# Two engine orders rewritten: gathers behind the products at a unit's begin, and the last tile's down product by halves

## The chip, the cores and the metric

The kernel runs on one core of one Trainium2 chip. The metric is the device time of one execution in microseconds; before the change it is 761.45, the median of three runs (758.97 to 761.66). The engines are TensorE (PE, whose weight loads are shown as PEld), VectorE (DVE), ScalarE (ACT), GpSimd (POOL) and SyncE (SP, which here only issues transfers).

## What is computed

The input X has 4 sequences of 2048 rows and 256 channels. Cut to what matters:

```python
xp = (X @ Wp + bp).reshape(B, T, 4, D)
f = (pos @ Wf + bf).reshape(T, 3, D)            # filters, from sines and cosines of the position
y = xp[:, :, 0]
for i in range(3):
    y = causal_fft_convolution(y, f[:, i]) * xp[:, :, i + 1]
x = layernorm(X + y)
h = silu(x @ wg.T) * (x @ wu.T)                 # weights are int32, scaled by 1/127
out = layernorm(x + h @ wd.T)
```

## The kernel before, in words

Time is cut into 16 blocks of 128 rows. **Projection**: 128 products (`project`, L398), 64 for each half of the output columns; DVE takes each out of PSUM (`collect`, L793 to L811), ScalarE and POOL split the inputs into a high and a low part. The gates of the three stages go to HBM and come back as tiles (`load_gate`).

**Convolution**: 12 units u (3 stages of 4 groups of 64 channels), each a loop over 16 blocks k (L549 for PE, L734 for ACT, L968 for DVE, L1062 for POOL). A convolution is a Toeplitz product within a block (`toeplitz`, L432 to L434, 8 groups q per unit, each in two halves of 12 small products), done one unit ahead, and a part from all earlier blocks: `state` (L411, three fp16 matmuls, accumulating over the blocks), `multiply` on DVE (L832, state times the filter's coefficients, into `prod`), and `readout` on PE (L452, four fp32 passes). `gather` on DVE (L857) adds two readouts to `y` and frees their PSUM bank; a unit has 8 gathers, numbered 0 to 7, and the last (of one block only) is number 7. `readout` of an odd block waits for the gather that frees its bank (`z_done`). `apply` on POOL (L1033) multiplies `y` by the gate, 9 times a unit. ScalarE makes the scaled copies of the next unit (`high`, L628 and L630), takes out Toeplitz results (`evacuate`, L636) and sums squares (`square`, L643) for the scale of a later unit; DVE makes the low fp16 half (`low`, L866) and, at block 3, the scale itself (`factors`, L815 to L824). PE's Toeplitz group q of the next unit waits for `low` of q and, at every even q, for the filter tile that SP loads (`load_filter`, L264, 1 MB, three slots).

The order of the work is written out by hand for each engine, and every engine runs its list in order. What each list has at a unit's begin: on PE at block 0 the last half Toeplitz group, state 0, readout 15 of the unit before; at block 1 state 1, a half group and the norm; at block 2 a half group, state 2, readout 1. On DVE gather 6 of the unit before comes at block 1 and gather 7 at block 3, both behind the multiply (L974 and L975), except in the last unit and behind it, where they come first in blocks 0 and 1. POOL's `apply` of the unit before follows the same places, and its first one of the new unit stands at block 4. SP's list per unit, for j = 0 to 3: a filter load that waits for a Toeplitz group, then the gate load of the next unit, which waits for squares at blocks 10 and 14 of this unit and 2 and 6 of the next (units 8 on: for `apply`, `gated`). In the unit before the last SP also loads the weights of the feed-forward part and the rows for the first addition.

At the end of the projection DVE's list is: collect 125, multiply 2 of unit 0, collect 126, collect 127; the first `low` of unit 1 follows as the first thing of the unit loop. Projections cycle through PSUM banks 2 to 5, of which readouts use 4 and 5.

**Feed-forward**: 16 tiles of 512 rows (128 rows of each of 4 sequences), 6 hidden blocks m each: gate and up product (L472), `silu` on ACT, `product` on DVE (L905), `high_h` on ACT, `low_h` on POOL (L1052), then the down product. For the last tile `down_last` (L499) loops over m outside and the four sequences b inside; its two halves (b 0 and 1, b 2 and 3) are in two banks and signal `d_done` as block 5 of each is through. Behind it DVE has, for each half, `sum2_half` (L910), `bn_stats` and `bn_aggr`; POOL's `root` (L1040) adds epsilon, negates the mean, takes the power -0.5 and multiplies; three rows are then normalised on ACT (L674), the last on DVE (L1020), and two transfers store the halves.

Of the kernel before, what the change touches and what calls it, by code (L numbers as in the profile page):

```python
# [11 lines left out]
ALU = mybir.AluOpType  # L12
# [3 lines left out]
NB, T, D = 4, 2048, 256  # L16
NS = 3
NA = T // P
# [4 lines left out]
NU = NS * NG  # L23
# [4 lines left out]
NPAIR = NA // 2  # L28
# [8 lines left out]
HM = HID // P  # L37
NTOK = NB * P
NSEG = 8
EPS = 1e-5  # L40
# [5 lines left out]
def program(nc, XT, X, WP, BP, WF, BFC, BFR, POSR, CM, CB, EF, EI, ONES, IDENT, WGT, WUT, WDT, OUT):  # L46
# [3 lines left out]
    with ExitStack() as ctx:  # L50
# [3 lines left out]
        def sem(name):  # L54
            return ctx.enter_context(nc.semaphore(name))
# [17 lines left out]
        mv = sb("mv", [P, 2, NB, 2])  # L73
# [116 lines left out]
        root_ready = sem("root_ready")  # L190
        rstd = sem("rstd")
        const_ready = sem("const_ready")
        x1n_ready = sem("x1n_ready")
        tr_done = sem("tr_done")
        xh_ready = sem("xh_ready")
# [57 lines left out]
        with nc.Block() as block:  # L253
# [134 lines left out]
            def _(pe):  # L388
# [54 lines left out]
                def readout(u, a):  # L443
                    n = u * NE + a - 1
                    m = u * NPAIR + (a - 1) // 2
                    e0 = NA - 1 - a if turned(u // NG) else a
                    half = (a - 1) % 2
                    if half == 0 and m >= 2:
                        pe.wait_ge(z_done, m - 1)
                    pe.wait_ge(mult_done, n + 1)  # L450
                    for h in range(2):
                        mm = pe.matmul(b_out[m % 2][:, half * W:(half + 1) * W], ei[:, h, e0 * P:(e0 + 1) * P],  # L452
                                       prod[:, n % 3, h, :], start=(h == 0), stop=(h == 1))
                    mm.then_inc(r_done, 1)
# [43 lines left out]

                def down_last(k):  # L499
                    pe.wait_ge(zz_ready, k * 2 + 1)  # L500
                    for m in range(HM):
                        pe.wait_ge(hh_ready, k * HM + m + 1)
                        if m < HM - 1:
                            pe.wait_ge(hl_ready, k * HM + m + 1)
                        else:
                            pe.wait_ge(hl_last, 1)
                        for b in range(NB):
                            for h in (hh, hl):
                                mm = pe.matmul(b_d[b // 2][:, (b % 2) * D:(b % 2 + 1) * D],  # L509
                                               h[:, k % 2, m, b * P:(b + 1) * P], wd[:, m, :],  # L510
                                               start=(m == 0 and h is hh and b % 2 == 0),
                                               stop=(m == HM - 1 and h is hl), skip_group_check=True)
                            if m == HM - 1 and b % 2:
                                mm.then_inc(d_done, 1)
# [272 lines left out]
            def _(dve):  # L787
# [166 lines left out]
                for n in range(NT):  # L954
                    collect(NT + n)
                    if n == 6:
                        factors(0)
                    if n == 9:
                        factors(1)
                    if n % 6 == 4 and 1 <= n // 6 <= NQ:  # L960
                        low(0, n // 6 - 1)
                    if n == 56:
                        dve.wait_ge(wfx_ready, 4 * NS)
                    if n in (57, 59, 61):
                        multiply(0, (n - 57) // 2)
                dve.wait_ge(x_lo, 2 * NT)
                dve.wait_ge(wfx_ready, 4 * NS)
                for u in range(NU + 1):  # L968
                    for k in range(NA):
                        if u >= NU - 1 and k <= 1:  # L970
                            gather(u - 1, NPAIR - 2 + k)
                        if k >= 5 and k % 2 and u < NU:
                            gather(u, (k - 5) // 2)
                        if k % 2 == 0 and u + 1 < NU:  # L974
                            low(u + 1, k // 2)  # L975
                        if u < NU and k < NE and (u or k >= 3):
                            multiply(u, k)
                        if k in (1, 3) and 1 <= u < NU - 1:
                            gather(u - 1, NPAIR - 2 + k // 2)
                        if k == 3 and u + 2 < NU:  # L980
                            factors(u + 2)
                        if u == NU - 1:
# [24 lines left out]
                for h in range(2):  # L1007
# [7 lines left out]
                    for b in (2 * h, 2 * h + 1):  # L1015
                        last = nc.vector.bn_aggr(mv[:, 0, b, :], bst[:, 0, b, :])
                    last.then_inc(mean_ready, 1)
                dve.wait_ge(rstd, 2 * NA + 1)
                dve.wait_ge(out_done[1], (NA // 2 - 1) * 16)
                nc.vector.tensor_scalar(oo[:, 1, NB - 1, :], zl[:, NB - 1, :], rs[:, 0, NB - 1:NB], nb[:, 0, NB - 1:NB],  # L1020
                                        ALU.mult, ALU.add).then_inc(oo_last, 1)

            @block.gpsimd
            def _(pool):
# [36 lines left out]
                                            ALU.subtract).then_inc(x_lo, 1)  # L1061
                for u in range(NU + 1):  # L1062
                    for k in range(NA):
                        if u >= NU - 1 and k <= 1:
                            apply(u - 1, NPAIR - 1 + k)
                        if k in (1, 3) and 1 <= u < NU - 1:
                            apply(u - 1, NPAIR - 1 + k // 2)
                        if k == (4 if u < NU - 1 else 2) and u < NU:
                            apply(u, 0)
                        if k >= 5 and k % 2 and u < NU:  # L1070
                            apply(u, (k - 3) // 2)
# [24 lines left out]
                        low_h(k, 5)  # L1096
                pool.wait_ge(oo_ready, (NA - 2) * NB + 1)
                root(1, count2(NA - 1))
                root(0, 2 * NA, slice(0, 2))
                root(0, 2 * NA + 1, slice(2, 4))  # L1100


def tables():
# [60 lines left out]
```

## Time and profile before

| | |
|---|---|
| median of three runs | 761.45 us |
| profiled execution | 759.56 us |
| its span, first to last instruction | 757.8 us |
| mean granted clock of PE | 0.994 of full |
| projection, units, feed-forward in the span | 0 to 200, 200 to 500, 500 to 758 |

How to read it: times in rows are microseconds from the span's start. A row of a timeline has start, duration, engine, line, operation, output and inputs with their sizes, a count, and in brackets the idle time before it with what ended it. PE rows show matmuls whose ends are modelled: their starts are good, their durations overlap. A clock of 1.00 is the upper of PE's two levels (2.4 GHz), 0.50 the lower (1.2 GHz).

### The profile page before, as it was taken

The numbers are of one execution on the slowest core, as the hardware profiler recorded it, in microseconds if no ns is written. First come the engines' busy times: TensorE is split into PE (matmuls) and PEld (weight loads), VectorE is DVE, ScalarE is ACT, GpSimd is POOL, SyncE is SP. The second block draws the span as 40 slices with busy tenths as digits, with TensorE's granted clock in tenths as the row PEclk, the third lists the DMA queues.
The fourth block names the chain that finished last, engine by engine and source line by source line (L and its number), as shares of the span: only waits on it lengthen the run. The fifth ranks groups of instructions, "written<-read, shape, count | busy, mean of one in ns | idle before, by whom it ended". The sixth has DMA issues, their size and how long they took to land.

```text
span 757.8 us, 16074 instructions
## 1 busy us (share of the span) xinstructions
PE 732.5 (97%) x5936; PEld 547.3 (72%) x5936; DVE 552.1 (73%) x1083; ACT 488.0 (64%) x962; POOL 421.3 (56%) x483
## 2 busy tenths in 40 slices
PE   6999999999999999999999999799999999999995
PEld 5878878888788888888888888555665556655663
DVE  4898778777788888888888888766656566565644
ACT  3445554444378888788877665456677776777753
POOL 3445554445244443444444434798788878888653
PEclk9999999999999999999999999999999999999998
DMA  8659668999899998999899996622435435442322
GB/s 301 214 177 337 241 216 283 317 319 309 278 277 263 256 267 245 260 258 262 250 247 270 304 264 212 225 57 57 108 88 123 101 89 108 95 128 57 64 55 78
DMA packets 193676, 152.69 MB, mean 202 GB/s; under 512 B 35776, under 2 KB 177216, under 8 KB 193344
## 3 DMA queue, kind: packets, MB, share of 16 engines
q1 hardware_dynamic: 191744, 146.36, 66.6%
q10 hardware_dynamic: 1856, 5.31, 2.1%
q8 instruction: 48, 0.79, 0.4%
q14 instruction: 28, 0.23, 0.1%
HBM read 109.45 MB, written 34.34 MB: 190 GB/s over the span
## 4 chain that ended last, share of the span: by engine, by line
PE 88%; DVE 4%; DMA 3%; ACT 2%; issue 2%; POOL 1%; SPq 0%; POOLq 0%; DVEq 0%; ACTq 0%
PE bank L398 22%; PE bank L472 21%; PE bank L452 19%; PE bank L493 10%; PE bank L411 7%; PE bank L432 3%; PE bank L433 3%; PE bank L434 3%; DMA toep<-filter_rows 1%; DMA wi<-in_WDT 1%; DVE y L857 1%; PE bank L509 1%; DVE wfx L844 1%; DVE prod L832 1%; DMA xt<-in_XT 1%
## 5 line engine op out<-in xcount | busy, mean ns | idle before, releaser
L1033 POOL TENSOR_TENSOR y<-y,gate 128x512 f32<-128x512 f32 (+1 forms) x108 | 124.4, 1157 | 170.2 <-DVE y L857 157.6
L398 PE MATMUL bank<-wps,xs 128*128 128x512 f32 x768 | 183.5, 398 | 7.8 <-DVE wps L790 6.6
L452 PE MATMUL bank<-prod,ei 128*128 128x256 f32 x720 | 188.0, 384 | 1.5 <-DVE y L857 1.5
L398 PEld LDWEIGHTS bank<-wps,xs 128*128 128x128 f32 x768 | 144.7, 190 | 39.4 <-POOL xs L1060 7.3
L832 DVE TENSOR_TENSOR prod<-bank,wfx 128x512 f32<-128x512 f32 x180 | 124.2, 690 | 43.7 <-PE bank L411 43.7
L1060 POOL TENSOR_TENSOR xs<-xt,xs 128x256 fp32r<-128x256 f32 x128 | 93.5, 742 | 101.2 <-ACT xs L607 101.2
L472 PE MATMUL bank<-xh,wq 128*128 128x512 f16 x384 | 145.7, 379 | 0.3 <-DVE hf L905 0.2
L472 PE MATMUL bank<-xl,wq 128*128 128x512 f16 x384 | 145.8, 380 | 0.0
L1052 POOL TENSOR_TENSOR hl<-hf,hh 128x512 f16<-128x512 f32 x95 | 110.7, 1168 | 53.1 <-ACT hh L671 53.1
L452 PEld LDWEIGHTS bank<-prod,ei 128*128 128x128 f32 x720 | 123.6, 192 | 15.7 <-DVE y L857 4.3
L636 ACT ACTIVATE y<-bank,iscl 128x512 f32<-128x512 f32 x96 | 66.0, 687 | 88.0 <-PE bank L434 87.8
L905 DVE SCALAR_TENSOR_TENSOR hf<-bank,sg 128x512 f32<-128x512 f32 x96 | 65.2, 680 | 52.8 <-PE bank L472 25.2
L607 ACT ACTIVATE xs<-xt 128x256 fp32r<-128x256 f32 x128 | 51.5, 414 | 70.7 <-PE bank L398 63.4
L671 ACT ACTIVATE hh<-hf 128x512 f16<-128x512 f32 x96 | 60.2, 627 | 52.2 <-DVE hf L905 52.2
L411 PE MATMUL bank<-yh,ef 128*128 128x256 f16 x360 | 89.0, 274 | 4.7 <-DVE prod L832 4.4
L432 PE MATMUL bank<-yh,toep 128*128 128x64 f16 x768 | 88.1, 193 | 1.8 <-issue 1.7
L434 PE MATMUL bank<-yh,toep 128*128 128x64 f16 x768 | 88.0, 193 | 0.0
L433 PE MATMUL bank<-yl,toep 128*128 128x64 f16 x768 | 87.9, 193 | 0.0
L433 PEld LDWEIGHTS bank<-yl,toep 128*128 128x128 f16 x768 | 70.5, 98 | 17.4 <-issue 0.3
L432 PEld LDWEIGHTS bank<-yh,toep 128*128 128x128 f16 x768 | 72.6, 99 | 11.0 <-issue 5.7
L493 PE MATMUL bank<-wq,hl 128*128 128x256 f16 x360 | 79.4, 273 | 0.0
L493 PE MATMUL bank<-wq,hh 128*128 128x256 f16 x360 | 79.4, 273 | 0.0
(81 smaller groups left out, 1219.7 us busy)
## 6 DMA issues: line engine op xcount, KB each, us to landing
toep<-filter_rows SPq DMA_DIRECT2D x43, 1024.0 KB, 7.8
gate<-gates SPq DMA_DIRECT2D x48, 512.0 KB, 3.9
xt<-in_XT SPq DMA_DIRECT2D x31, 512.0 KB, 5.2
gates<-st SPq DMA_DIRECT2D x24, 512.0 KB, 4.1
gates<-toep SPq DMA_DIRECT2D x24, 512.0 KB, 4.0
xr<-in_X SPq DMA_DIRECT2D x16, 512.0 KB, 4.7
out_x<-oo SPq DMA_DIRECT2D x15, 512.0 KB, 3.2
toep<-filter_rows SPq DMA_DIRECT2D x10, 512.0 KB, 6.0
```

Of the source, the lines that this page charges most:

```text
L398: mm = pe.matmul(b_proj[n % PBK][:, :], xs[:, n % XSS, hx, k, :], wps[:, hw, k, p * 512:(p + 1) * 512], start=(k == 0 and q == 0), stop=(k ...
L411: mm = pe.matmul(b_state[:, 0:W], ef[:, e0, e, :], v[u % 2][:, k, :], start=(k == 0 and q == 0), stop=(k == NE - 1 and q == 2), skip_group ...
L432: pe.matmul(dst, lag[:, 0], yh[u % 2][:, :, cols], start=True, stop=False)
L433: pe.matmul(dst, lag[:, 0], yl[u % 2][:, :, cols], start=False, stop=False)
L434: mm = pe.matmul(dst, lag[:, 1], yh[u % 2][:, :, cols], start=False, stop=True)
L452: mm = pe.matmul(b_out[m % 2][:, half * W:(half + 1) * W], ei[:, h, e0 * P:(e0 + 1) * P], prod[:, n % 3, h, :], start=(h == 0), stop=(h == 1))
L472: mm = pe.matmul(dst[:, :], wt[:, t, m * P:(m + 1) * P], v[:, k % 2, :, t, :], start=(t == 0 and v is xh), stop=(t == KT - 1 and v is xl))
L493: mm = pe.matmul(b_d[b // 2][:, (b % 2) * D:(b % 2 + 1) * D], h[:, k % 2, m, b * P:(b + 1) * P], wd[:, m, :], start=(m == 0 and h is hh), ...
L832: nc.vector.tensor_tensor(prod[:, n % 3].rearrange("p r (c b) -> p r c b", b=NB), b_state[:, 0:W].rearrange("p (c b) -> p c b", b=NB).unsq ...
L1033: nc.gpsimd.tensor_tensor(y[:, u % NG, a:a + count, :], y[:, u % NG, a:a + count, :], gate[:, a:a + count, :], ALU.mult).then_inc(gated, 1)
L1052: nc.gpsimd.tensor_tensor(hl[:, k % 2, m, :], hf[:, m % 3, :], hh[:, k % 2, m, :], ALU.subtract).then_inc(hl_ready, 1)
L1060: nc.gpsimd.tensor_tensor(xs[:, n % XSS, 1], src, xs[:, n % XSS, 0].bitcast(F32), ALU.subtract).then_inc(x_lo, 1)
```

## The change

It touches four places. In PE's `readout` the first two of all wait for the projection's banks. In `down_last` blocks 0 to 2 go as before, over all four sequences; blocks 3 to 5 go for sequences 0 and 1, then for 2 and 3. On DVE gathers 6 and 7 stand behind the multiplies of blocks 0 and 1 in every unit, the first `low` of unit 1 moves to the end of the projection, between multiply 2 and collect 126, and in the last tile DVE adds epsilon for each half and normalises the last row as (x - mean) * rstd. POOL's `apply` follows: both of the old unit at blocks 0 and 1, the first of the new one at block 2; in the last tile it takes the power first, then negates the mean.

```diff
@@ readout
                     if half == 0 and m >= 2:
                         pe.wait_ge(z_done, m - 1)
+                    if half == 0 and m < 2:
+                        pe.wait_ge(proj_used, 2 * NT - 1 + m)
@@ down_last
-                    for m in range(HM):
+                    for m, bs in [(m, range(NB)) for m in range(3)] + [(m, range(2 * h, 2 * h + 2)) for h in range(2)
+                                                                      for m in range(3, HM)]:
...
-                        for b in range(NB):
+                        for b in bs:
@@ DVE, second half of the projection
                     if n in (57, 59, 61):
                         multiply(0, (n - 57) // 2)
+                    if n == 61:
+                        low(1, 0)
@@ DVE, units
-                        if u >= NU - 1 and k <= 1:
-                            gather(u - 1, NPAIR - 2 + k)
                         if k >= 5 and k % 2 and u < NU:
                             gather(u, (k - 5) // 2)
-                        if k % 2 == 0 and u + 1 < NU:
+                        if k % 2 == 0 and u + 1 < NU and u + k:
                             low(u + 1, k // 2)
                         if u < NU and k < NE and (u or k >= 3):
                             multiply(u, k)
-                        if k in (1, 3) and 1 <= u < NU - 1:
-                            gather(u - 1, NPAIR - 2 + k // 2)
+                        if k <= 1 and u >= 1:
+                            gather(u - 1, NPAIR - 2 + k)
@@ DVE, last tile, in the loop over the halves and behind it
                     last.then_inc(mean_ready, 1)
-                dve.wait_ge(rstd, 2 * NA + 1)
+                    dve.wait_ge(mean_ready, 2 * NA + h)
+                    nc.vector.tensor_scalar(rs[:, 0, 2 * h:2 * h + 2], mv[:, 0, 2 * h:2 * h + 2, 1], EPS, None,
+                                            ALU.add).then_inc(var_last, 1)
+                dve.wait_ge(root_last, 2)
                 dve.wait_ge(out_done[1], (NA // 2 - 1) * 16)
-                nc.vector.tensor_scalar(oo[:, 1, NB - 1, :], zl[:, NB - 1, :], rs[:, 0, NB - 1:NB], nb[:, 0, NB - 1:NB],
-                                        ALU.mult, ALU.add).then_inc(oo_last, 1)
+                nc.vector.tensor_scalar(oo[:, 1, NB - 1, :], zl[:, NB - 1, :], mv[:, 0, NB - 1, 0:1], rs[:, 0, NB - 1:NB],
+                                        ALU.subtract, ALU.mult).then_inc(oo_last, 1)
@@ POOL, units
-                        if u >= NU - 1 and k <= 1:
+                        if k <= 1 and u >= 1:
                             apply(u - 1, NPAIR - 1 + k)
-                        if k in (1, 3) and 1 <= u < NU - 1:
-                            apply(u - 1, NPAIR - 1 + k // 2)
-                        if k == (4 if u < NU - 1 else 2) and u < NU:
+                        if k == 2 and u < NU:
                             apply(u, 0)
@@ POOL, last tile
-                root(0, 2 * NA, slice(0, 2))
-                root(0, 2 * NA + 1, slice(2, 4))
+                pool.wait_ge(mean_ready, 2 * NA)
+                for h in range(2):
+                    rows = slice(2 * h, 2 * h + 2)
+                    pool.wait_ge(var_last, h + 1)
+                    nc.gpsimd.tensor_tensor(rs[:, 0, rows], rs[:, 0, rows], mhalf[:, rows], ALU.pow).then_inc(root_last, 1)
+                    nc.gpsimd.tensor_tensor(nb[:, 0, rows], mv[:, 0, rows, 0], minus[:, rows], ALU.mult).then_inc(neg_last, 1)
+                    pool.wait_ge(root_last, h + 1)
+                    pool.wait_ge(neg_last, h + 1)
+                    nc.gpsimd.tensor_tensor(nb[:, 0, rows], nb[:, 0, rows], rs[:, 0, rows], ALU.mult).then_inc(rstd, 1)
```

## Rows read from the trace of the kernel before

**Rows 1.** The page: busy time of PE and its share of the span

```profile
PE 732.5 (97%) x5936; PEld 547.3 (72%) x5936; DVE 552.1 (73%) x1083; ACT 488.0 (64%) x962; POOL 421.3 (56%) x483
```

**Rows 2.** Who waited for whom, PE: us in total, times, longest

```profile
PE bank L411 <- DVE prod L832: 4.4, 4, 1.6
...
PE bank L452 <- DVE y L857: 1.5, 10, 0.2
```

**Rows 3.** Timeline of PE and DVE at the boundary of unit 4

```profile
300.22 0.69 DVE L832 TENSOR_TENSOR prod<-bank,wfx 128x512 f32<-128x512 f32 x1
...
301.51 0.69 DVE L832 TENSOR_TENSOR prod<-bank,wfx 128x512 f32<-128x512 f32 x1 [0.59 <-PE bank L411]
...
302.11 0.74 DVE L857 SCALAR_TENSOR_TENSOR y<-bank,iscl,y 128x512 f32<-128x512 f32 x1
...
302.48 0.27 PE L411 MATMUL bank<-yh,ef 128*128 128x256 f16 x1
...
302.91 1.13 PE L452 MATMUL bank<-prod,ei 128*128 128x256 f32 x4 [0.15 <-DVE y L857]
...
305.76 0.16 DVE L815 TENSOR_REDUCE total<-bank 128x1 f32<-128x8 f32 x1
...
306.87 0.68 DVE L832 TENSOR_TENSOR prod<-bank,wfx 128x512 f32<-128x512 f32 x1
...
307.38 0.19 PE L434 MATMUL bank<-yh,toep 128*128 128x64 f16 x1
307.61 0.28 PE L411 MATMUL bank<-yh,ef 128*128 128x256 f16 x1
```

**Rows 4.** Timeline, a filter load and the first product that uses it

```profile
298.77 1.43 SPq L264 DMA_DIRECT2D toep<-filter_rows  x1
...
307.05 0.19 PE L432 MATMUL bank<-yh,toep 128*128 128x64 f16 x1
```

**Rows 5.** Line L264: issues at 206.17, at 274.04, and 34 from 224

```profile
DMA to landing us min/median/max: 7.7/7.7/7.7
...
DMA to landing us min/median/max: 8.4/8.4/8.4
...
DMA to landing us min/median/max: 6.7/7.8/10.2
```

**Rows 6.** Timeline of DVE, PE and SP at the begin of unit 0

```profile
201.00 0.67 DVE L866 TENSOR_TENSOR yl<-bank,yh 128x512 f16<-128x512 f32 x1
...
201.77 0.19 PE L432 MATMUL bank<-yh,toep 128*128 128x64 f16 x1 [1.72 <-issue]
...
203.13 0.69 DVE L866 TENSOR_TENSOR yl<-bank,yh 128x512 f16<-128x512 f32 x1 [1.46 <-ACT yh L630]
...
206.17 0.36 SPq L264 DMA_DIRECT2D toep<-filter_rows  x1
...
214.56 0.19 PE L432 MATMUL bank<-yh,toep 128*128 128x64 f16 x1
```

**Rows 7.** Windows: length, busy time of each engine, granted clock, DMA share, GB/s

```profile
202.50:206.00 3.50, 3.50 (x32) 2.83 (x29) 0.69 (x1) 2.59 (x4) 0.00 (x0) 0.51 0.98 313
```

**Rows 8.** Timeline of the last tile's end

```profile
749.48 0.69 DVE L910 SCALAR_TENSOR_TENSOR x<-bank,x1n 128x512 f32<-128x512 f32 x1 [0.59 <-PE bank L509]
...
753.26 0.69 POOL L1045 TENSOR_TENSOR rs<-rs,mhalf 128x2 f32<-128x2 f32 x1
...
754.26 0.60 ACT L674 ACTIVATE oo<-x,nb,rs 128x256 f32<-128x256 f32 x1 [0.50 <-POOL nb L1048]
754.27 0.41 DVE L1020 TENSOR_SCALAR oo<-x,rs,nb 128x256 f32<-128x256 f32 x1 [1.38 <-POOL nb L1048]
```

**Rows 9.** POOL's low half of the hidden block: one instruction, then the page's group

```profile
515.89 1.45 POOL L1052 TENSOR_TENSOR hl<-hf,hh 128x512 f16<-128x512 f32 x1 [0.65 <-ACT hh L671]
...
L1052 POOL TENSOR_TENSOR hl<-hf,hh 128x512 f16<-128x512 f32 x95 | 110.7, 1168 | 53.1 <-ACT hh L671 53.1
```

**Rows 10.** The chain that ended last: start, length, what

```profile
476.45 8.26 DMA wi<-in_WDT
```

More of the change, by code:

```diff
@@ L192, in program @@
         const_ready = sem("const_ready")
+        var_last = sem("var_last")
+        neg_last = sem("neg_last")
+        root_last = sem("root_last")
         x1n_ready = sem("x1n_ready")
```

## The prediction, made before the changed kernel was run

> **What bounds the kernel.** Three views, in this order. The page first: TensorE (PE) has matmuls open during 97% of the span [rows 1], so the change can only gain where PE stands still. Then the list of who waited for whom, on PE alone: the longest sum that this change touches is small. Ten times PE waited, 0.2 us at most, for a gather (`y` L857), and four times for a product (`prod` L832) [rows 2]. Those sums undercount, since ends of matmuls are modelled; so I read the third view, the timeline, from start to start: matmuls of 256 fp16 columns follow each other by 0.11 us when nothing is in the way, and any larger distance is a stall.
>
> One boundary of units, that of unit 4, shows the pattern [rows 3]. The third matmul of state 2 starts at 302.48, the first readout at 302.91: 0.43 where 0.11 is normal, so **0.32 us idle**. What released it is the gather issued at 302.11, 0.80 before. The second stall is at the fifth block: the twelfth product of a Toeplitz group starts at 307.38, the state behind it at 307.61, **0.20 idle** (products of 64 columns are 0.03 apart); it starts 0.74 behind the multiply of 306.87, which VectorE (DVE) reached late because gather, four scale instructions (from 305.76, half a microsecond together) and a low part lay before it. A third idle of 0.07 stands in front of the Toeplitz group at 307.05 [rows 4]. That is 0.6 us in each of about nine boundaries; the tenth (unit 10) has no scale instructions and only the first stall.
>
> **The boundary after the change.** Gather 6 is issued behind multiply 0: 300.22 + 0.60 (the distance from multiply to gather, 301.51 to 302.11) = 300.82, so the readout could start at 301.6 and no longer waits: it starts when the state is through, at 302.59. The gather lasts 0.74 and lets the next instruction in about 0.07 before its end, at 301.49; multiply 1 starts at 301.51, when its state is there. It slips by nothing, but the margin is 0.02. Gather 7 goes from block 3 to block 1, behind multiply 1, at 302.12 and takes 0.4; the low part behind it starts at 302.5 where it was 302.77; multiply 2 at 303.11, and state 3 must stand 0.75 behind it, 303.86, where PE would be there at 303.80: **0.06 given back**. Multiply 3 is then followed by the scale instructions at 305.0 (before 305.7), low part 2 at 305.5 and multiply 4 at 306.11: state 5 can start at 306.96, 0.65 before the old 307.61. So 0.65 for a boundary, if nothing else is late. GpSimd (POOL) gets its gate products over block 0 and 1 and the one of block 0 follows at block 2; it idles for most of a unit, and the squares of ScalarE that need them come at blocks 4 and 6, so I cost this at nothing. If that cover went, a late square would delay a load on SP (last unit, below).
>
> **What is late next: the filter load.** The load that the Toeplitz group of block 5 needs is issued by SP at block 14 of the unit before, ahead of everything that gets faster (298.77), and is used at 307.05 [rows 4], 8.28 later. PE would now be there 0.44 earlier, 7.84 after the issue. Landings of such loads take 6.7 to 10.2, median 7.8, and the one issued at 274.04 took 8.4 [rows 5]. So in about half of nine boundaries the load is the last to come. Four at a mean wait of 0.4: 1.6 off. Nine times 0.65 less 1.6, plus 0.28 for unit 10, is **4.5 us**. Bounds: 9 x 0.65 + 0.3 = 6.1 with no wait, and 1.0 if every load takes 8.4.
>
> **The begin of unit 0.** The low part of the first block of unit 1 stands behind the last two collects: 201.00; PE idles 1.72 us for it [rows 6], and the granted clock then falls to half (mean 0.51) for 3.4 us [rows 7]. Moved ahead of the last two collects it runs at about 198.6 (its fp16 half is there long before). It delays the collect of tile 126 by 0.4 us; the last collect still starts at 200.1, when its matmuls end, so nothing behind it (stores on SP, the high part of the second block on ScalarE) moves. PE goes on without a break with both half groups, the norm and a readout (1.8 us, to 201.7). The new wait on the projection's banks ends at 200.2, in time. Then the next low part is the one that is late: it comes at 203.13 now, because ScalarE's high part waited for the first low part and would now wait only for the last collect (201.2); I get 202.6 and a new stall of 1.7 us to 203.3. So the stall is moved, not removed; 1.4 us is won here, and the half clock's 1.7 as well if it stays away. But PE cannot keep that: the filter for block 9 is issued at 206.17, behind the last stores, takes 7.7 (213.87) [rows 5, 6], and was used at 214.56. All that gets through is the slack of 0.6 us. **0.6 us**; bounds 0.2 (that load as slow as 8.1) and 1.9 (that load comes early as well). Whether the clock falls again behind a stall of 1.7 therefore hardly counts: a stall of 1.6 by the waits elsewhere [rows 2] left it full, one of 1.72 [rows 6] did not, and the block-9 wait of 1.3 us would absorb most of its price.
>
> **The last tile.** The first half of the down product ends 0.9 us earlier, but DVE takes it up only when the statistics before it are through, at 748.9 instead of 749.48 [rows 8]: 0.6. The added epsilon instruction between the halves costs 0.2 (a dependent small instruction). 0.4 arrives at the second half, epsilon on DVE instead of POOL is a trade of equals; on POOL the power (0.69, at 753.26) moves to 752.8, the negated mean now follows it, and the last product is at 753.7. ScalarE's last row starts at 753.93 instead of 754.26; it is free at 753.77, so this is nearly its floor. DVE's row starts behind the power, 753.5, and isn't last. **0.3 us.** The second half's own matmuls end when they did; the low half of block 5, which half one now needs earlier, is ready 0.8 us before that.
>
> A rule speaks against this place. What the trace shows: the POOL product that ran beside a DVE instruction with two inputs in SBUF (`low_x`, L897) took 1.45 us, where the mean of its kind is 1.17 [rows 9], a stretch of 0.3. In the new tail DVE's row (0.41 [rows 8]) runs beside POOL's last small product, which ScalarE's row needs; before, they did not meet. A stretch of 0.3 would leave 0.05 of the 0.3 us; that is the lower bound. The Trainium skill, "SBUF — State Buffer", section "SBUF: two separate sides", calls the port pair that DVE and GpSimd share an exclusive lock held for the whole instruction, while the other one blocks; by it POOL's product waits out the DVE row and the tail gains 0.1, the sum 5.2 instead of 5.4. The row of this trace shows stretching, not blocking.
>
> **The sum.** 4.5 + 0.6 + 0.3 = 5.4 us. The profiled execution took 759.56 (span 757.8 and 1.8 around it), and 754.2 is what it becomes. The median of the runs shown is 761.45, 1.9 above it; less 5.4 this is **756.1 us**.
>
> **The rivals.** (a) *The loads take back what the boundaries give.* If most take 8.2 or more, a boundary is worth 0.3 or less: 2.5 in all plus 0.9, less what block 13 loses, so 3 us, 758.5. For: DMA engines are busy nine tenths of these stretches; against: median 7.8. (b) *The new order on DVE costs what it frees*: the margin at multiply 1 is 0.02; if the gather keeps DVE 0.3 longer there (its PSUM read held), state 2 is as late as the readout was, and the boundaries give 0.2 each for the shorter queue at block 5; with tail and begin 2.5 or less, 759.5. For: everything hangs on back-to-back distances; against: they repeat to 0.01 in all ten boundaries. (c) *Slower*: the landing time grows, because a shorter unit puts the same bytes closer together. Place: block 5 of units 1 to 8; it decides from a landing of 8.5, where a boundary has nothing left; at the 10.2 that the range shows [rows 5], each of eight loses 10.2 - 7.84 - 0.65 = 1.7, 13.7 us, less 1.8 for the rest: 773; at 9.2, 0.7 each, 765. Against: only the stretch where loads pile up showed such times. The Trainium skill, "DMA: Bandwidth & Descriptors", section "Latency and other measured facts", says that access to HBM goes from 0.2 us to 2 at high load; by it such growth is possible, and no row here tells its size. (d) *The weights come late in the last unit*: there gather 6 moves behind multiply 0 and gather 7 behind multiply 1, POOL's products end 1.1 us later, SP's last gate load waits for them, and the down weights behind it are on the chain that ends last (8.26 us to landing from 476.45 [rows 10]). They queue behind other loads of weights and rows, so a later issue should be hidden; uncovered it costs 1.0: 757.1. (e) *The cap at the begin isn't there* or fewer loads are late: 7.2 us, 754.2. (f) *The half product doesn't come early at all*: 0.3 less, inside the range.
>
> **Numbers.** Half a per cent, 3.8 us, is what a measurement of this kernel can tell. Forecast with (d) inside it 0.55, (e) 0.07: faster by more than that, 0.62. (a) 0.20 and (b) 0.12 lie within it, and a little of (c): 0.33. (c) beyond it 0.05. The range goes from (e), 754.2, to (b) with most of tail and begin lost, 760.2.
>
> **What would show it.** Right: no readout behind a wait for L857 at the boundaries, and units of 24.1 instead of 24.7 us, some with PE waiting for `toep<-filter_rows` at block 5; the first Toeplitz group right behind the projection; new waits in front of the second group and at block 9; last ScalarE row 0.3 earlier. Wrong: unit lengths unchanged with a multiply released late, loads of unit 1 to 8 landing after 8.5 us, or the begin gaining its whole 2 us.

## The result, and the profile after

The changed kernel takes 756.06 us (median of 7 runs, 754.61 to 757.54), the kernel before in the same comparison 761.02 (7 runs). The ratio is 0.9938, interval 0.9923 to 0.9953: **5.0 us or 0.6% faster**. Forecast were 756.1 us and 5.4 us less.

The profiled execution is one of the slower ones of its kernel, 757.46, and that of before was one of its faster ones, 759.56. The two traces therefore differ by 2.1 us only (spans 755.7 and 757.8), and a stretch of one trace can't be set against the other without knowing how much it changes from one execution to the next. Cut at the same events (the end of the projection is taken 0.23 us behind the start of its last matmul; state 1 of a unit is the matmul group of its block 1):

| stretch, us | before | after | forecast |
|---|---|---|---|
| projection | 199.88 | 199.81 | same |
| its end to state 1 of unit 1 (the begin) | 26.92 | 28.97 | -0.6 |
| state 1 of unit 1 to state 1 of unit 11 | 246.96 | 243.09 | -4.5 |
| from there to the start of the last matmul | 275.84 | 275.65 | same |
| last matmul's start to the span's end | 8.15 | 8.14 | -0.3 |

In these two traces the boundaries gained most of what was forecast, the begin lost 2 us, and the tail did nothing. The page of after, PE:

```profile
PE 727.5 (96%) x5936; PEld 544.8 (72%) x5936; DVE 552.1 (73%) x1085; ACT 487.9 (65%) x962; POOL 420.8 (56%) x481
```

Matmuls are open for 5 us less [rows 1], for the same 5936. About 2 of the 5 lie in the window of [rows 7]: open for all of its 3.50 us at half clock before, and for 1.41 after, where PE stands idle for the rest (last section). So this sum is no measure of the gain. Next, who waited for whom on PE (us in total, times, longest):

```profile
PE bank L435 <- DMA toep<-filter_rows: 3.3, 6, 1.1
PE bank L435 <- DVE yl L872: 2.1, 1, 2.1
PE bank L435 <- issue: 1.1, 1, 1.1
```

The ten waits of the readout for a gather (`y` L857 in [rows 2]) are gone. Loads of filters stand in their place, and two stalls for low parts at the begin. The boundary of unit 4 in the timeline of DVE, PE and SP, with the filter load that it uses (compare [rows 3, 4]):

```profile
300.09 1.44 SPq L267 DMA_DIRECT2D toep<-filter_rows  x1
...
301.54 0.69 DVE L838 TENSOR_TENSOR prod<-bank,wfx 128x512 f32<-128x512 f32 x1
302.15 0.74 DVE L863 SCALAR_TENSOR_TENSOR y<-bank,iscl,y 128x512 f32<-128x512 f32 x1
302.83 0.69 DVE L838 TENSOR_TENSOR prod<-bank,wfx 128x512 f32<-128x512 f32 x1
...
306.31 0.16 DVE L821 TENSOR_REDUCE total<-bank 128x1 f32<-128x8 f32 x1
...
307.42 0.68 DVE L838 TENSOR_TENSOR prod<-bank,wfx 128x512 f32<-128x512 f32 x1
...
308.43 0.20 PE L435 MATMUL bank<-yh,toep 128*128 128x64 f16 x1 [0.35 <-DMA toep<-filter_rows]
```

The gather sits right behind multiply 0 (0.61 later), multiply 1 follows 1.29 behind multiply 0, as it did before: the margin of 0.02 held. The tiny reduction of the scale is 4.77 behind multiply 0 where it was 5.54 in [rows 3], and multiply 4 is 5.88 behind instead of 6.65: 0.77 less. A unit in which PE waits for no load now takes 24.06 us, where units took 24.72; but in this boundary the load issued 8.34 before is the last to come, and PE stands 0.35.

The stretch of the table's third row, in the timeline of PE after the change: state 1 of unit 1 and state 1 of unit 11, 243.09 us apart:

```profile
228.78 0.28 PE L414 MATMUL bank<-yh,ef 128*128 128x256 f16 x1
...
471.87 0.28 PE L414 MATMUL bank<-yh,ef 128*128 128x256 f16 x1
```

The same two rows before, 246.96 apart:

```profile
226.80 0.28 PE L411 MATMUL bank<-yh,ef 128*128 128x256 f16 x1
...
473.76 0.28 PE L411 MATMUL bank<-yh,ef 128*128 128x256 f16 x1
```

The begin of unit 0, timeline of DVE, PE and SP after the change (compare [rows 6]):

```profile
197.84 1.99 DVE L815 TENSOR_TENSOR toep<-bank,bp 128x512 f32<-128x512 f32 x2 [2.41 <-DMA gates<-toep]
...
199.68 0.68 DVE L838 TENSOR_TENSOR prod<-bank,wfx 128x512 f32<-128x512 f32 x1
...
200.27 0.68 DVE L872 TENSOR_TENSOR yl<-bank,yh 128x512 f16<-128x512 f32 x1
200.87 2.03 DVE L815 TENSOR_TENSOR toep<-bank,bp 128x512 f32<-128x512 f32 x2
201.05 0.19 PE L435 MATMUL bank<-yh,toep 128*128 128x64 f16 x1 [1.08 <-issue]
...
205.25 0.19 PE L435 MATMUL bank<-yh,toep 128*128 128x64 f16 x1 [2.09 <-DVE yl L872]
...
207.48 0.36 SPq L267 DMA_DIRECT2D toep<-filter_rows  x1
...
215.84 0.20 PE L435 MATMUL bank<-yh,toep 128*128 128x64 f16 x1 [1.13 <-DMA toep<-filter_rows]
```

The same place on DVE in the trace of before:

```profile
195.99 2.07 DVE L809 TENSOR_TENSOR toep<-bank,bp 128x512 f32<-128x512 f32 x2 [0.48 <-DMA gates<-toep]
...
200.09 1.06 DVE L809 TENSOR_TENSOR toep<-bank,bp 128x512 f32<-128x512 f32 x1 [0.32 <-PE bank L398]
```

The forecast had the moved low part at 198.6, and the last collect at 200.1, unmoved. Here the low part runs at 200.27, and the last two collects behind it from 200.87 on. The first row makes the difference. The collects before them waited 2.41 us for the store of the gates (`gates<-toep`), where the same instruction waited 0.48 before. So the collects run back to back right into unit 0, without the gap of 0.32 that stood before the last one, and the low part put between them moves the last two back by its own 0.6.

SP issues the filter load for block 9 once the last store of the gates has landed, so it follows them. Counted from the projection's end it goes out at 7.67, before at 6.29; it lands 8.3 us later instead of 7.7, and the group of block 9 starts at 16.03 instead of 14.68. That is 1.35 of the 2.05 that the begin got longer; the rest comes behind block 9, 0.52 of it as a wait for the next filter load.

### The profile page after: what moved, and what is told of

The parts are those of the page before. It is cut to its first block, busy times and chain, and to the rows that moved or that the text cites. A ratio compares the mean times of both kernels' runs of the same rounds, so it can differ in the third digit from the quotient of the medians.

```text
span 755.7 us, 16080 instructions
## 1 busy us (share of the span) xinstructions
PE 727.5 (96%) x5936; PEld 544.8 (72%) x5936; DVE 552.1 (73%) x1085; ACT 487.9 (65%) x962; POOL 420.8 (56%) x481
## 4 chain that ended last, share of the span: by engine, by line
PE 81%; DMA 9%; DVE 4%; ACT 2%; issue 2%; POOL 1%; SPq 0%; ACTq 0%; POOLq 0%; DVEq 0%
PE bank L477 20%; PE bank L401 20%; PE bank L457 16%; PE bank L498 10%; PE bank L414 6%; DMA toep<-filter_rows 6%; PE bank L435 3%; PE bank L436 3%; PE bank L437 3%; DMA gates<-toep 1%; DMA xt<-in_XT 1%; DMA wi<-in_WDT 1%; DVE wfx L850 1%; DMA toep<-in_WP 1%; DVE toep L815 1%
## 5 line engine op out<-in xcount | busy, mean ns | idle before, releaser
L457 PE MATMUL bank<-prod,ei 128*128 128x256 f32 x720 | 186.0, 381 | 0.0
```

## The experiments

**Two parts, each alone, against the whole.** First: only the gathers' and POOL's new order.

```diff
 # kernel before, DVE
-                        if u >= NU - 1 and k <= 1:
-                            gather(u - 1, NPAIR - 2 + k)
...
-                        if k in (1, 3) and 1 <= u < NU - 1:
-                            gather(u - 1, NPAIR - 2 + k // 2)
+                        if k <= 1 and u >= 1:
+                            gather(u - 1, NPAIR - 2 + k)
@@ POOL
-                        if u >= NU - 1 and k <= 1:
+                        if k <= 1 and u >= 1:
                             apply(u - 1, NPAIR - 1 + k)
-                        if k in (1, 3) and 1 <= u < NU - 1:
-                            apply(u - 1, NPAIR - 1 + k // 2)
-                        if k == (4 if u < NU - 1 else 2) and u < NU:
+                        if k == 2 and u < NU:
                             apply(u, 0)
```

> The kernel before with only the order of gathers and gate products at the units' begins changed. Theory G (the boundaries carry the change): about 4 us faster than before (the changed kernel's trace has its states 1 of units 1 and 11 at a distance of 243.1 us instead of 247.0), so a ratio near 0.995; the distance is again 243 to 243.5. Rival: the three parts add up only together, and this alone gives 2 us or less.

Measured: 755.75 us, ratio 0.9936 (0.9919 to 0.9952), the whole change's 0.9938. The boundaries stretch is 242.66 us in its trace. **The gathers are the whole gain**, as far as the intervals tell (each about 1.2 us to either side).

Then the changed kernel with the low part put back:

```diff
 # changed kernel
-                    if n == 61:
-                        low(1, 0)
-                        if k % 2 == 0 and u + 1 < NU and u + k:
+                        if k % 2 == 0 and u + 1 < NU:
```

> The changed kernel with the first low part of unit 1 back behind the last collects. Theory as predicted: 0.6 us slower than the changed kernel, PE idle about 1.7 us before the first Toeplitz group and the clock at half once. Rival, from the changed kernel's trace, where collect 124 waited 2.4 us for a store of gates and the moved low part pushed collect 127 by 0.6 us: the move is worth nothing or costs up to 0.6 us, so this kernel is as fast or faster by 0.5 us.

Measured: 755.55 us, ratio 0.9924 (0.9899 to 0.9949): with the low part in its old place no loss shows. Its begin took 28.30 us in the trace, that of the gathers alone 27.40. And from the other side, the kernel before with the low part moved and nothing else:

```diff
 # kernel before
                     if n in (57, 59, 61):
                         multiply(0, (n - 57) // 2)
+                    if n == 61:
+                        low(1, 0)
@@ units
-                        if k % 2 == 0 and u + 1 < NU:
+                        if k % 2 == 0 and u + 1 < NU and u + k:
@@ readout
+                    if half == 0 and m < 2:
+                        pe.wait_ge(proj_used, 2 * NT - 1 + m)
```

> The kernel before with only the first low part of unit 1 moved to the projection's end and PE's new waits. Predicted 0.6 us faster. Rival, from the traces since (27.1 to 27.6 us from the projection's end to state 1 of unit 1 with the move, 26.9 to 28.3 without): worth nothing, 0 plus or minus 0.5 us, with PE's stall moved from the first Toeplitz group to the second and to block 9.

Measured: 760.65 us, ratio 0.9995 (0.9983 to 1.0006), a gain of 0.4 us with an interval from a loss of 0.5 to a gain of 1.3. **No gain of the move shows**, but by the timed runs alone the 0.6 of the forecast isn't excluded. The timeline of DVE in its trace shows the same order as after, in a milder case:

```profile
197.10 1.98 DVE L811 TENSOR_TENSOR toep<-bank,bp 128x512 f32<-128x512 f32 x2 [1.00 <-DMA gates<-toep]
...
199.52 0.68 DVE L868 TENSOR_TENSOR yl<-bank,yh 128x512 f16<-128x512 f32 x1
200.11 2.04 DVE L811 TENSOR_TENSOR toep<-bank,bp 128x512 f32<-128x512 f32 x2
```

The low part and the last two collects follow each other by 0.59. The wait for the store of the gates lasted 0.5 us in the trace of before, 2.4 in that of after, and 0.5 to 1.9 in eleven of the twelve experiments (in the last, with the low part already moved ahead of it, there was none); only at the low end is there a gap for the low part to hide in. The traces show no gain either, sorted by the length of that wait: where it was 0.5 us, the begin took 26.92 without the move and 27.30 with it; around 1.1, 26.88 without and 27.07 and 27.19 with; from 1.5 to 1.9, 27.40 and 28.30 without and 27.63 and 28.15 with. Each is one trace of a kernel that differs elsewhere too, so this is weaker than it looks.

**Is the filter load what limits the boundaries now?** SP issues filter loads in the order of use, but each behind a load of gates that waits for ScalarE's squares, and these for POOL. Theory: SP's place in its own queue, not the transfer, makes the load late; so issue each filter one place earlier.

```diff
 # changed kernel, SP
                 load_gate(0, 3)
+                sp.wait_ge(toep_done, 2 * NSUB + 2)
+                load_filter(NSUB + TSLOT)
                 for u in range(NU):
...
-                        s = NSUB * (u + 1) + j
+                        s = NSUB * (u + 1) + j + 1
```

> The changed kernel, SP issues each filter load ahead of the gate load that it stood behind (some 3 us earlier, the same bytes). Theory L (at block 5 the late issue of the filter load is what PE waits for): all waits of PE on toep<-filter_rows in units 1 to 10 go (2.5 us in the changed kernel's trace), the distance from state 1 of unit 1 to that of unit 11 is 240.6, 2.5 us faster than the changed kernel. Rival D (the DMA engines are full, so an earlier issue only queues): landings get longer by what the issue is earlier, or the gate loads come late, gain under 0.5 us.

Measured: 754.37 us, ratio 0.9909 (0.9892 to 0.9926), 1.7 us under the changed kernel by the medians; the two intervals just overlap, so the stretch of the units in the trace has to decide. The timeline of PE:

```profile
227.01 0.28 PE L416 MATMUL bank<-yh,ef 128*128 128x256 f16 x1
...
467.62 0.28 PE L416 MATMUL bank<-yh,ef 128*128 128x256 f16 x1
```

240.61 us for ten units, ten times the 24.06 of a unit that waits for nothing. The view of waits has no row for PE in that stretch. For the same stretch of the changed kernel it has one (total, times, longest; from start to start these waits cost 2.5 us):

```profile
PE bank L435 <- DMA toep<-filter_rows: 1.7, 4, 0.7
```

The loads themselves land sooner: the line of the filter loads in the experiment, its 34 issues from 224 on:

```profile
DMA to landing us min/median/max: 6.2/7.2/8.6
```

The same line in the changed kernel, 35 issues:

```profile
DMA to landing us min/median/max: 6.7/7.8/9.2
```

In the experiment's timeline of SP the filter load now goes out between the gate loads, 1.5 to 1.8 us behind the last one, where it was 0.4 (299.69 and 300.09 after). The load for block 5 is issued 12.7 us ahead of its use (median of ten units), where it was 8.3:

```profile
296.60 0.36 SPq L274 DMA_DIRECT2D gate<-gates  x1
298.12 0.36 SPq L267 DMA_DIRECT2D toep<-filter_rows  x1
302.00 0.36 SPq L274 DMA_DIRECT2D gate<-gates  x1
```

The four kernels with this edit on top of the new gathers had 240.60 to 240.63 in this stretch, seven with the new gathers and the old filters 241.6 to 243.2, mean 242.4. So the same edit on the kernel before should be worth nothing, if the gathers' stalls were the limit there and the load only the one behind it:

> The kernel before with filter loads ahead of gate loads, gathers in their old place. Theory L with G (two limits behind each other: first the gather and the queue on DVE, 7.8 to 8.3 us behind the issue the load): alone it takes away only PE's few waits on loads of before, at most 0.9 us by the idle of 0.07 to 0.26 in front of Toeplitz groups; units 246 to 246.5 us instead of 247.0. Rival: late loads cost as much before as after, 2 us off here too.

Measured: 759.54 us, ratio 0.9982 (0.9969 to 0.9995), and 247.00 us for the ten units where the kernel before had 246.96. The row of its waits on PE for the gather:

```profile
PE bank L454 <- DVE y L859: 1.6, 10, 0.2
```

The ten waits for the gather are all there (ten times 0.16); the only two for filter loads, 1.0 us together, lie at the begin of unit 0. The expectation of 246 to 246.5 missed: there was nothing to take away here. **One limit stands behind the other**: the gathers' order alone is worth about 5 us, the filters' order alone nothing in the units (0.2% in all; where from wasn't found), both together 6.4 in the units.

**What holds the begin?** First, the low part two tiles earlier, at n == 59, ahead of the crowded collects.

```diff
 # changed kernel
-                    if n == 61:
+                    if n == 59:
                         low(1, 0)
```

> The changed kernel with the first low part of unit 1 two tiles earlier, behind multiply 1 of unit 0, where DVE then waits for the store of gates anyway (0.5 us in the trace of before, 2.4 in the changed one). If the moved low part costs by delaying collects 126 and 127: up to 0.6 us faster than the changed kernel, the last collect 0.5 us earlier against collect 124. Rival: the begin is set by when the stores land, whatever stands on DVE; no difference beyond 0.3 us.

Measured: 755.03 us, ratio 0.9926 (0.9910 to 0.9943), against 0.9938 no difference clear of the noise. The first group of unit 1 now follows the projection without a gap (0.01 us behind it, 1.24 in the trace of after, though 0.00 also in that of the low part moved alone), but block 9's group starts 14.76 behind the projection, where it was 14.68 before and 16.03 after. Then also the wait of ScalarE on the last collect moved behind its high part, so that the second low part is early:

```diff
 # on top of the last one, ScalarE
-                act.wait_ge(proj_used, 2 * NT)
                 for u in range(NU + 1):
                     for k in range(NA):
+                        if u == 0 and k == 2:
+                            act.wait_ge(proj_used, 2 * NT)
```

> The kernel with the low part two tiles earlier, and ScalarE's wait for the last collect moved from ahead of the unit loop to its block 2, so that the high part of the second block no longer waits for it. Theory C (the filter load for block 9, issued behind the last stores, caps the begin): the second low part comes about 3 us earlier, the stall of 2.1 us before the second Toeplitz group goes, and the same time reappears as a longer wait of PE on toep<-filter_rows at block 9; total unchanged within 0.5 us. Rival: the stall before the second group is what costs, and its 2 us come off the total.

Measured: 755.18 us, ratio 0.9925 (0.9911 to 0.9938). Waits of PE over the whole trace:

```profile
PE bank L435 <- DMA toep<-filter_rows: 3.4, 3, 2.7
...
PE bank L435 <- DVE yl L873: 0.3, 1, 0.3
```

The wait for the second low part fell from 2.1 us (1.8 without ScalarE's edit) to 0.3, and the wait for block 9's filter grew from 1.1 (1.4) to 2.7; the group of block 9 starts 14.56 behind the projection, 0.2 earlier than without ScalarE's edit. That is the cap that the forecast spoke of, shown: **what is won ahead of block 9 is taken by the filter load issued behind the last stores.**

There was a price on top. Behind the wait of 2.73 the granted clock fell to half for 3.4 us, as the windows view shows (columns as in [rows 7]; packets are counted whole where they start, so a share can pass 1):

```profile
214.20:217.70 3.50, 3.50 (x24) 2.75 (x22) 1.29 (x2) 0.57 (x1) 0.00 (x0) 0.51 1.17 331
```

From the group of block 9 to state 1 of unit 1 it then took 13.89 us, and 12.33 where the clock stayed up (the low part earlier, without ScalarE's edit): 1.6 us lost. Both with the filters ahead:

> Low part two tiles earlier, ScalarE's wait moved, and filter loads ahead of gate loads, on the changed kernel. Theory L: state 1 of unit 1 to that of unit 11 again 240.6 us as with the filters ahead alone, and 753.5 to 754.5 us in total. Rival: with the begin shorter the loads bunch up in unit 0 and the units lose up to 1 us again.

Measured: 754.33 us, ratio 0.9913 (0.9899 to 0.9926), against 0.9909 of the filters alone. The begin changes add nothing there either; in this trace too the clock fell behind block 9's wait (2.26 us), and the same stretch took 13.96.

**POOL's order alone put back**, on the changed kernel:

> The changed kernel with GpSimd's gate products in the old order (the old unit's at blocks 1 and 3, the new unit's first at block 4), gathers on DVE as changed. Predicted: GpSimd's order costs and gives nothing, the units take 24.06 us plus waits on filter loads as in the changed kernel. Rival: its order is part of the gain (squares and loads behind it come later without it), units longer by 0.2 us or more, 2 us in all.

Measured: 754.37 us in the one run, units 242.36, inside the spread of the others. It costs and brings nothing that one run can tell.

**What holds the tail?** The store of tile 14, half a megabyte, is still under way when the last rows' stores go out. Theory: the queue of stores sets the end, not the last row's arithmetic.

```diff
 # changed kernel, SP, in store(k)
+                    if k == NA - 2:
+                        for h in range(2):
+                            sp.wait_ge(oo_ready, k * NB + 2 * h + 3)
+                            sp.dma_start(oview[:, k, 2 * h:2 * h + 2], oo[:, k % 2, 2 * h:2 * h + 2]).then_inc(out_done[k % 2], 16)
+                        return
@@ SP, at the end
-                sp.wait_ge(out_done[0], NA // 2 * 16)
+                sp.wait_ge(out_done[0], NA // 2 * 16 + 16)
```

> The changed kernel with the store of the last but one tile in two transfers, the first as soon as its two rows are normalised (1 us earlier). Theory S (in all six traces the end comes 4.9 to 5.0 us after that store's issue, whatever the last row does: the end is set by the store queue's 1 MB): from the last matmul to the end 7.8 us or less instead of 8.13. Rival: the end is the last store's issue plus its 2.7 us to landing, nothing changes.

Measured in one run: 755.69 us; in its trace last matmul to the end is 7.58 us, the eleven traces with that store whole have 8.12 to 8.16. Last matmul, then SP's issues, then the span's end at 753.9:

```profile
746.31 0.27 PE L520 MATMUL bank<-wq,hl 128*128 128x256 f16 x1
...
748.54 1.35 SPq L362 DMA_DIRECT2D out_x<-oo  x2
...
750.50 1.12 SPq L371 DMA_DIRECT2D out_x<-oo  x2
```

The first half goes out 1 us earlier, and the end comes 0.56 us sooner, though the very last store is issued at the same place (4.95 behind the last matmul, as after). The other way round, that last store goes out 0.34 earlier after the change than before, and the end doesn't move. **While tile 14 is stored whole, its store sets the end.** Whether the shorter arithmetic counts once it is split wasn't run.

**Together.** Filters ahead and the split store on the changed kernel:

> The changed kernel with filter loads ahead of gate loads and the store of the last but one tile by halves. Both effects add: units 240.6 us, tail 7.6 us from the last matmul; 2.0 + 0.5 us off the changed kernel, 753.5 us. Rival: one hides the other or run-to-run movement of the begin swallows them, not below 754.3.

Measured: **752.91 us, ratio 0.9889 (0.9870 to 0.9908)**, 3.1 us under the changed kernel by the medians, and the best of all (that is more than the two parts of 1.8 and 0.56 that the traces show; the median of the kernel before alone moved by 0.3 from one comparison to the next). Timeline of PE, state 1 of unit 1, of unit 11, and the last matmul (span 752.1):

```profile
228.14 0.28 PE L421 MATMUL bank<-yh,ef 128*128 128x256 f16 x1
...
468.76 0.28 PE L421 MATMUL bank<-yh,ef 128*128 128x256 f16 x1
...
744.48 0.27 PE L522 MATMUL bank<-wq,hl 128*128 128x256 f16 x1
```

240.62 for the units and 7.58 for the tail: both parts arrive in full. With the two begin edits on top:

> As the one with filters ahead and store halves, and low part two tiles earlier with ScalarE's wait moved. The begin gave nothing in earlier runs, so the same as without these two, within 0.5 us. Rival: with the filter loads no longer queued behind gate loads the earlier begin comes through, 1 us faster than without.

Measured: 753.87 us, ratio 0.9900 (0.9883 to 0.9917), not better.

## Why the prediction was right, and where it wasn't

**Boundaries, forecast 4.5: right, by its own steps.** (Units here are the ten from state 1 of unit 1 to state 1 of unit 11.) Removing both stalls gives 0.66 a unit (24.72 to 24.06), worked out as 0.65; the 0.02 of margin at multiply 1 held, so rival (b) fell. Without load waits the ten units gain 246.96 - 240.61 = 6.35, where the step without loads had 6.1. The late loads took 2.5 of it in the trace of after (units of 24.50, 24.95 and twice 24.58, the others within 0.1 of 24.06) against the 1.6 forecast; over seven traces the mean is 242.4, that is 1.8 for the loads and 4.5 for the gain. By the timed runs of the gathers alone it is 5.1 us. That rival (a) had the right mechanism is shown by the filters issued ahead; its size was the forecast's, not the rival's. Landings did not grow (6.7 to 9.2, median 7.8; [rows 5]), so rival (c) had no ground.

**Begin, forecast 0.6: not found.** Alone the move measured a gain of 0.4 us, with an interval from -0.5 to 1.3, and the begins in the traces are no shorter with it. The step that failed is "the last collect still starts at 200.1, when its matmuls end, so nothing behind it [...] moves", and with it the 7.7 us for the landing of the filter load for block 9. Both were read from one execution. The collects wait for the store of the gates, 0.5 to 2.4 us, in most traces long enough that they run back to back; then the low part delays the last ones and the stores behind them. With the low part moved alone the last stores went out at 2.06 behind the projection's end instead of 1.65. They landed sooner, so the filter load was issued at the old place (6.32, before 6.29), but it took 8.48 to land, not 7.7: PE stood 1.36 for it, and the group of block 9 came at 14.85 instead of 14.68. In the six traces with the low part between the collects this load took 8.0 to 8.5 us to land, in the four with it behind them 7.6 to 8.3; why it lands later wasn't found. So the slack of 0.6 that the forecast let through was gone. The cap itself was right: where the stall for the second low part was taken away, the wait at block 9 took it up. The bounds (0.2 to 1.9) excluded a zero.

The forecast also said that a second fall of the clock "hardly counts", since the wait at block 9 would absorb it. That holds for a fall ahead of that wait; where the clock fell behind it, it cost 1.6 us.

**Tail, forecast 0.3: wrong, it is under 0.1.** The step that failed is that the end follows ScalarE's last row. The timeline of the tail after the change, with the SP issues:

```profile
747.52 0.27 PE L515 MATMUL bank<-wq,hl 128*128 128x256 f16 x1
...
750.61 0.70 POOL L1110 TENSOR_TENSOR rs<-rs,mhalf 128x2 f32<-128x2 f32 x1 [0.60 <-DVE rs L1025]
750.74 0.37 SPq L360 DMA_DIRECT2D out_x<-oo  x1
751.34 0.41 DVE L1029 TENSOR_SCALAR oo<-x,mv,rs 128x256 f32<-128x256 f32 x1 [0.81 <-POOL rs L1110]
751.61 0.20 POOL L1114 TENSOR_TENSOR nb<-nb,rs 128x2 f32<-128x2 f32 x1
...
751.72 1.12 SPq L366 DMA_DIRECT2D out_x<-oo  x2
751.84 0.60 ACT L680 ACTIVATE oo<-x,nb,rs 128x256 f32<-128x256 f32 x1
```

And before, the last matmul and SP's issues:

```profile
749.60 0.27 PE L509 MATMUL bank<-wq,hl 128*128 128x256 f16 x1
...
752.81 0.37 SPq L357 DMA_DIRECT2D out_x<-oo  x1
753.79 1.47 SPq L363 DMA_DIRECT2D out_x<-oo  x2
```

The arithmetic did what was worked out: ScalarE's last row starts 4.32 behind the last matmul, before it was 4.66, so 0.34 earlier. The last store went out 0.34 earlier with it, as the shorter pair of SP issues shows (1.12 for 1.47). But the end is 4.9 behind SP's issue of tile 14's store (750.74, span 755.7), as it was before (752.81, span 757.8), and that store goes out 3.2 behind the last matmul in both. The missing step is the question what is late next **on the transfers**; the split store answered it. The bound below nothing was missing too.

On the pair of POOL and DVE the forecast read [rows 9] as "stretching, not blocking", which the row doesn't show. The DVE instruction beside it, from the trace of before:

```profile
514.84 1.48 DVE L897 SCALAR_TENSOR_TENSOR xln<-x1n,xhn 128x1024 f16<-128x1024 f32 x1 [0.20 <-ACT xhn L661]
```

It ended 0.43 us behind the start of POOL's product, which took 0.29 longer than the median of its kind (1.45 for 1.16). In 13 other tiles the two overlap by 0.18, and the product takes 0.04 longer. And this DVE instruction itself, which began 0.40 before an earlier product of POOL ended, took 0.25 longer than usual (1.48 for 1.23). Each time the second one is longer by the overlap less some 0.14, which is what waiting for the other's end would give as well. The Trainium skill, "SBUF — State Buffer", section "SBUF: two separate sides", would have the later one blocked; these rows agree with it. In the new tail DVE's row and POOL's small product overlap by 0.14 only (751.61 to 751.75), and the product took its usual 0.20: too short an overlap to tell.

**The last unit, rival (d): didn't come.** From state 1 of unit 11 to the last matmul it is 275.65, before 275.84.

**The total.** The forecast gain is 0.4 from the measured one, the forecast time 0.04. It came out near since one large term was right and the two wrong ones were small: 0.9 us forecast, about 0 measured. The 1.9 between the profiled execution of before and its median was taken over whole and fitted. So close a time is luck: the interval of the gain alone runs from 3.6 to 5.9 us.

## What to carry to other kernels

When two stalls on the bottleneck go, look for the transfer that was already in its place when they ended, and at its place in the queue of the engine that issues it: moving the filter load ahead of a gate load that waits cost nothing and gave another 1.8 us in the units (6.4 instead of 4.5). A step put "into a gap" must hold in more than one execution: a gap behind a wait for a store is there in some and not in others. At the end of a kernel follow the last stores as well as the last arithmetic: half a microsecond lay in splitting one store, none in shortening the arithmetic while that store was whole.

## What the runs showed of the hardware

The granted clock at the begin. It fell to half for 3.4 us in six of the fourteen traces, each time behind an idle of PE: before (1.72 us idle, [rows 7]), the gathers alone (2.20), the low part put back (2.26), filters and store together (2.11), and twice behind the wait at block 9 (2.73 and 2.26). It stayed up behind idles of much the same length in the other eight: 1.72 in the kernel before with the filters ahead, 1.61, 1.80 and 1.96 in three, and 2.09 to 2.17 in four. After the change PE idles twice, 1.08 and 2.09 us, and the clock stays at its upper level. The same stretch in the windows view (length, busy time of each engine, granted clock, DMA share, GB/s):

```profile
202.50:206.00 3.50, 1.41 (x20) 0.99 (x19) 1.08 (x2) 2.72 (x5) 0.00 (x0) 1.00 0.68 257
```

And in the kernel before with the filters ahead, behind its idle of 1.72:

```profile
202.20:205.70 3.50, 3.39 (x50) 2.73 (x49) 1.76 (x7) 2.56 (x5) 0.00 (x0) 1.00 1.00 327
```

So the length of one idle doesn't decide it; what does wasn't found. Nor does a fall always cost: the trace of before, with the fall ahead of block 9, has one of the shortest begins of all (26.92, and 26.88 in the trace with the filters ahead, without a fall), since the load for block 9 caps it either way. Behind block 9 a fall cost 1.6 us.

The begin takes 26.9 to 29.0 us over the traces, and it goes with how long the collects wait for one store (0.5 us at 26.9, 2.4 at 29.0) and with falls of the clock behind block 9; ten units that wait for no load take 240.60 to 240.63 in four kernels.

The kernel before with the low part moved had 247.98 in the units, 1.0 more than before, nearly all of it in two of them (25.62 and 24.83 us), with two waits for filter loads (0.9 us together), though nothing there was changed. Why wasn't found.
